# Three reordered steps and a new placement of TensorE's operands in a two-layer graph network kernel

## What is computed

```python
h = relu(layernorm(x))
# layer 0: attention over the graph, then K = 3 hops
Xw = h @ Wv + bv
e  = leaky_relu((Xw @ aw[:d])[:, None, :] + (Xw @ aw[d:])[:, :, None] + ab, 0.2)
A  = adj * exp(e);  T = A / (A.sum(-1, keepdims=True) + 1e-12)
H  = h @ Wk[0] + (T h) @ Wk[1] + (T T h) @ Wk[2] + bk.sum(0)
x  = x + relu(H)
# layer 1: three graph convolutions
h = relu(layernorm(x))
y = relu(adj @ (h @ W1) + b1)
y = relu(adj @ (y @ W2) + b2)
x = x + adj @ (y @ W3) + b3
```

## The kernel before

| product | what moves | starts at | stationary | starts at |
|---|---|---|---|---|
| z1 | m | 0 | w_gcn0 | 64 |
| p2 | w_p2, 258 columns wide | 0, 32 (second half 8, 40) | h0T | 64 |
| z3 | s3 | 0 | adjT | 64 |
| ay | y1 | 0 | aT | 0 |
| s2, s3 | w_gcn1, w_gcn2 | 64 | y | 0 |
| p01 | w_p01 | 64 | h0T | 64 |
| z2 | adjT_full | 64 | s2 | 0 |
| ap | p2, 258 columns wide | 0, 32, 64, 96 | aT | 0 |
| m | adjT_full | 64 | h1 | 64 |

## Time and profile before

### The profile page before, as it was taken

The page is one execution under the profiler, slowest core; times in us unless marked ns, Lnnn a source line. Parts: engine busy times, 40 slices in busy tenths (PEclk is TensorE's granted clock), DMA queues, the critical chain, the costliest instruction groups (busy, mean ns, idle before and its releaser), DMA issues.

```text
span 865.4 us, 21032 instructions
## 1 busy us (share of the span) xinstructions
PE 846.4 (98%) x6236; PEld 794.7 (92%) x6236; DVE 728.3 (84%) x2001; ACT 683.7 (79%) x1671; POOL 509.3 (59%) x593
## 2 busy tenths in 40 slices
PE   6899999999999999999999999999999999999996
PEld 5799999999999999999999999999999999999995
DVE  4788888888888888888888888888888888888872
ACT  4688888888888888888888887887888888888773
POOL 3555655655655655665665665665665665665652
PEclk9999999999999999999999999999999999999999
DMA  8153343343343443443343344334334334334101
GB/s 201 35 119 80 98 99 84 97 97 82 99 97 81 101 95 82 100 96 87 96 95 91 93 94 94 89 94 93 91 94 98 87 92 100 84 94 99 45 25 37
DMA packets 245488, 78.19 MB, mean 90 GB/s; under 512 B 202368, under 2 KB 237312, under 8 KB 245376
## 3 DMA queue, kind: packets, MB, share of 16 engines
q1 hardware_dynamic: 244288, 75.81, 37.2%
q10 hardware_dynamic: 1088, 1.05, 0.4%
HBM read 44.04 MB, written 32.77 MB: 89 GB/s over the span
## 4 chain that ended last, share of the span: by engine, by line
PE 94%; DMA 1%; POOL 1%; issue 1%; DVE 1%; ACT 1%; SPq 0%; ACTq 0%; DVEq 0%; POOLq 0%
PE bank L950 45%; PE bank_p L950 35%; PE bank_turned L950 7%; PE bank_T L950 5%; PE bank_T L971 2%; DMA w_raw<-in_L_gnn_Wk 1%; POOL w_gcn_lo L420 0%; DMA h_blocks<-h_rows 0%; PE bank_p L1127 0%; POOL w_p_lo L415 0%; POOL rstd L376 0%; SPq L307 0%; SPq L286 0%; DVE y_full L767 0%; ACT y_full L604 0%
## 5 line engine op out<-in xcount | busy, mean ns | idle before, releaser
L385 POOL TENSOR_TENSOR y__lo<-y_full,y__hi 128x256 fp32r<-128x256 f32 x256 | 183.3, 736 | 159.6 <-ACT y_full L604 159.6
L376 POOL TENSOR_TENSOR rstd<-veps,minus_half 128x2 f32<-128x2 f32 x128 | 111.5, 871 | 180.2 <-DVE veps L682 174.0
L950 PE MATMUL bank_p<-w_p_hi,h0T_hi 128*128 128x258 f32 (+1 forms) x512 | 175.7, 359 | 1.0 <-ACT h0T_hi L502 0.7
L950 PE MATMUL bank_p<-w_p_lo,h0T_hi 128*128 128x258 f32 (+1 forms) x512 | 165.0, 338 | 0.0
L950 PE MATMUL bank_p<-w_p_hi,h0T_lo 128*128 128x258 f32 (+1 forms) x512 | 141.8, 338 | 0.0
L950 PE MATMUL bank<-w_gcn_hi,y__hi 128*128 128x256 f32 x512 | 130.9, 291 | 1.6 <-ACT y__hi L604 1.3
L950 PE MATMUL bank<-w_gcn_lo,y__hi 128*128 128x256 f32 x512 | 124.7, 279 | 0.0
L604 ACT ACTIVATE y__hi<-bank,bias_col 128x256 fp32r<-128x256 f32 x256 | 119.6, 467 | 3.0 <-PE bank L950 3.0
L604 ACT ACTIVATE y_full<-bank,bias_col 128x256 f32<-128x256 f32 x256 | 120.4, 470 | 0.0
L950 PEld LDWEIGHTS bank_p<-w_p_hi,h0T_hi 128*128 128x128 f32 x512 | 96.6, 189 | 7.1 <-ACT h0T_hi L502 0.9
L950 PEld LDWEIGHTS bank_p<-w_p_lo,h0T_hi 128*128 128x128 f32 x512 | 96.8, 189 | 5.8
(11 more groups left out here) (95 smaller groups left out, 2300.2 us busy)
## 6 DMA issues: line engine op xcount, KB each, us to landing
x_in<-in_x SPq DMA_DIRECT2D x64, 256.0 KB, 3.1
x_new<-x_out SPq DMA_DIRECT2D x64, 256.0 KB, 2.2
h_rows<-h SPq DMA_DIRECT2D x61, 256.0 KB, 2.0
h_blocks<-h_rows SPq DMA_DIRECT2D x244, 64.0 KB, 2.5
adj_blocks<-in_adj SPq DMA_DIRECT2D x256, 32.0 KB, 2.0
w_raw<-in_L_gnn_Wk ACTq DMA_DIRECT2D x3, 256.0 KB, 7.1
w_raw<-in_L_gnn_W SPq DMA_DIRECT2D x3, 256.0 KB, 6.2
bk_bc<-in_L_gnn_bk SPq DMA_DIRECT2D x1, 384.0 KB, 5.9
```

The lines of the kernel that those rows point to most:

```text
L376: pool.tensor_tensor(rstd[n][k % 2][:], veps[n][k % 2][:], minus_half[:], ALU.pow)\
L385: pool.tensor_tensor(y[n][1][:, c], y_full[n][:, c], plain(y[n][0][:, c]), ALU.subtract)\
L950: return pe.matmul(dst, stationary, moving, start=start, stop=stop, skip_group_check=True)
```

## The change

It moves steps in three engines' `one`, and it allocates SBUF in another order. Semaphores and their waits, the instructions and their sizes stay the same.

- GpSimd: `adjT_low` goes from the end of the iteration (for pair i) to behind `power(1, b)`, one iteration later for the same pair.
- ScalarE: `norm(b)` goes ahead of `aT_high(a)`.
- VectorE: `p2_low(a)`, which stood between the wait and the work of `moments(1, b)`, goes behind `guard_variance(1, b)`; `shift(1, b)` goes ahead of `attention(a)`; `turn_adj` is done one pair ahead, behind `finish(d)`, just before `guard_sum(a)`.
- SBUF: every tensor that moves through TensorE in a product starts at 0 modulo 128 bytes, every stationary one at 64. w_p2 and p2 are padded from 258 to 288 columns (`WIDE`), so that their halves start there too; the products still read 258. Two unused tensors fill up to the boundaries, and `scratch`, an output nobody reads, gives its room away (the dot products write into `x_out`'s buffers, early on).

```diff
+WIDE = D + P // 4
...
         ident = sb("ident", [P, P])
+        sb("up_to_a_kilobyte", [P, 3 * P // 4])
...
+        w_gcn = [None] + [hilo(f"w_gcn{n}", [P, C, D]) for n in range(1, K)]
+        w_p01 = hilo("w_p01", [P, C, 2 * D])
+        y1 = slots_hilo(2, "y1_", [P, G, D])
+        m = hilo("m", [P, C, G, P])
+        s3 = hilo("s3", [P, G, D])
+        adjT_full = [sb(f"adjT_full{n}", [P, G, P]) for n in range(4)]
+        w_p2 = hilo("w_p2", [P, C, WIDE])
+        p2 = slots_hilo(2, "p2_", [P, G, WIDE])
+
+        sb("half_a_block", [P, P // 8])
+        w_gcn[0] = hilo("w_gcn0", [P, C, D])
+        h0T = slots_hilo(2, "h0T", [P, G, C, P])
+        s2 = sb("s2", [P, G, D])
+        y = [hilo(f"y{n}_", [P, C, G, P]) for n in range(2)]
+        h1 = [sb(f"h1_{n}", [P, G, D]) for n in range(2)]
+        aT = slots_hilo(2, "aT", [P, G, P])
+        adjT = slots_hilo(4, "adjT", [P, G, P])
...
                 if b is not None:
                     power(1, b, k - LAG_B)
+                    adjT_low(b, (k - LAG_B) % ROUND)
...
-                if (n := here(i, 0)) is not None:
-                    adjT_low(n, k)
...
-                if a is not None:
-                    aT_high(a, k)
                 if b is not None:
                     norm(b, kb)
+                if a is not None:
+                    aT_high(a, k)
...
-                    moments(1, b, kb, lambda: p2_low(a, k) if a is not None else None)
+                    moments(1, b, kb, lambda: None)
                     guard_variance(1, b, kb)
-                elif a is not None:
+                if a is not None:
                     p2_low(a, k)
-                if a is not None:
+                if second(i):
                     turn_adj(a, k)
-                if a is not None:
-                    attention(a, k)
                 if b is not None:
                     shift(1, b, kb)
+                if a is not None:
+                    attention(a, k)
...
                     finish(d, kd)
+                if nxt is not None:
+                    turn_adj(nxt, kn)
```

More of the change, by code:

```diff
@@ L68, in gnn_kernel, with slots_hilo @@
         ident = sb("ident", [P, P])
+        sb("up_to_a_kilobyte", [P, 3 * P // 4])
+        def slots_hilo(n, name, shape):
+            return [hilo(f"{name}{s}", shape) for s in range(n)]
+        w_gcn = [None] + [hilo(f"w_gcn{n}", [P, C, D]) for n in range(1, K)]
[14 more added lines that the diff above has]
+        adjT = slots_hilo(4, "adjT", [P, G, P])
         w_raw = sb("w_raw", [P, 2 * K, C, D])
         wv_raw = sb("wv_raw", [P, C, D])
-        w_p2 = hilo("w_p2", [P, C, D + 2])
-        w_p01 = hilo("w_p01", [P, C, 2 * D])
-        w_gcn = [hilo(f"w_gcn{n}", [P, C, D]) for n in range(K)]
         wva = sb("wva", [P, C, 2])
@@ L129, in gnn_kernel @@
         x1 = slots(2, "x1_", [P, G, D])
-        m = hilo("m", [P, C, G, P])
-        s2 = sb("s2", [P, G, D])
-        s3 = hilo("s3", [P, G, D])
         y_full = [sb(f"y_full{n}", [P, C, G, P]) for n in range(2)]
-        y = [hilo(f"y{n}_", [P, C, G, P]) for n in range(2)]
         def bank(name):
@@ L630, in one @@
                     p1_copy(a, k, 0)
+                if b is not None:
+                    norm(b, kb)
                 if a is not None:
                     aT_high(a, k)
-                if b is not None:
-                    norm(b, kb)
                 if c is not None:
@@ L832, in dot @@
             def dot(dst, a, b, junk, signal):
[L834 removed]
+                dve.tensor_tensor_reduce(x_out[junk // G][:, junk % G, :], a, b, 1.0, 0.0, ALU.mult, ALU.add, dst)\
                    .then_inc(signal, 1)
@@ L899, in one @@
                     x1_statistics(b, kb)
-                    moments(1, b, kb, lambda: p2_low(a, k) if a is not None else None)
+                    moments(1, b, kb, lambda: None)
                     guard_variance(1, b, kb)
-                elif a is not None:
+                if a is not None:
                     p2_low(a, k)
-                if a is not None:
+                if second(i):
                     turn_adj(a, k)
+                if b is not None:
+                    shift(1, b, kb)
                 if a is not None:
                     attention(a, k)
-                if b is not None:
-                    shift(1, b, kb)
                 if i == 1:
@@ L988, in h_low_ready, with times_weights @@
                     pe.wait_ge(hT_lo, i - ON_TENSOR + 1)
-            def times_weights(hT, rows, w, dst, starts, passes=(False, True)):
+            def times_weights(hT, rows, w, cols, dst, starts, passes=(False, True)):
                 steps = [(g, c, a, b) for low in passes for g in range(G) for c in range(C)
@@ L995, in times_weights @@
                     start = c == 0 and a == HI and b == HI and g in starts
-                    last = matmul(dst[g], rows(hT[a], g, c), w[b][:, c, :], start, a == LO and c == C - 1)
+                    last = matmul(dst[g], rows(hT[a], g, c), w[b][:, c, 0:cols], start, a == LO and c == C - 1)
                 return last
@@ L1003, in p2_product @@
                     h_low_ready(i)
-                    times_weights(h0T[k % 2], graph_first, w_p2, dst, range(G), (True,)).then_inc(p2_done, 1)
+                    times_weights(h0T[k % 2], graph_first, w_p2, D + 2, dst, range(G), (True,)).then_inc(p2_done, 1)
                     return
@@ L1010, in p2_product @@
                     pe.wait_ge(y1_made, i)
-                times_weights(h0T[k % 2], graph_first, w_p2, dst, range(G), (False,))
+                times_weights(h0T[k % 2], graph_first, w_p2, D + 2, dst, range(G), (False,))
             def p01_product(i, k, g, chunks=range(C)):
@@ L1036, in ap_product @@
                     for g in range(G):
-                        last = matmul(bank_p2[:, g, 0:D + 2], aT[k % 2][a][:, g, :], p2[k % 2][b][:, g, :],
+                        last = matmul(bank_p2[:, g, 0:D + 2], aT[k % 2][a][:, g, :], p2[k % 2][b][:, g, 0:D + 2],
                                       (a, b) == (HI, HI), a == LO)
```

18 lines of the change are left out of this document (4 added, 14 removed).

## The result

The changed kernel takes **843.65 us** (median of 4 runs, 841.58 to 845.46). The kernel before, run beside it, takes 866.88 (4 runs, 865.77 to 868.97). The ratio is 0.973, with a 95% interval of 0.970 to 0.976. The forecast was 845.

A forecast was written before the change was run, and what follows sets the result against it. TensorE, busy all 12.92 us of an iteration, was the bound, then a ring through aT_hi and ap. Saving 0.17 (s3's wait) and 0.19 (placement) gave 12.56 us; 22.0 us over 61 iterations gave 845 us, range 820 to 861.

The forecast's parts named there:

- the ring: Chain hb, variance, norm, aT_hi, ap, m, s3, z1, p2, z3, ay, hb, forecast to bound the iteration at 12.56 us.
- The cost of nothing: GpSimd: moved `adjT_low` (0.73) falls into 2.44 us of idle time, so it costs nothing.
- `stats` at 1.88: VectorE: `stats` starts 1.88 us after `hb`, starting the times that put `nshift` at 3.96 and ap at 5.82.
- s2's wait: TensorE in s2 waits 0.24 us for y's low part; it goes, but merely becomes a wait for `aT_hi`.
- s3's wait: TensorE in s3 waits 0.17 us for y's low part; it goes, since that part comes 0.30 sooner.
- The term of 0.39: TensorE: opposite 64-byte halves for operands speed up fp32r matmuls by 0.39 us an iteration, 0.19 of it in the ring.
- no ring: Rival: the ring does not close, so TensorE's full 0.80 us an iteration counts; 818 us, chance 0.12.
- no placement: Rival: the new SBUF starts do nothing, so only 0.17 us an iteration is saved; 856 us, chance 0.18.
- a slack of about 0.6 against 0.7: Attention branch: `aT_hi` comes 0.7 us later where slack was about 0.6; the argument against "no ring".
- everything: Rival: placement gives its full gain, the ring saves 0.67 and the second ring, saving 0.63, binds; 829 us, chance 0.14.
- the second ring: Ring through y's low part and s3's low pass, saving 0.30 + 0.15 + 0.18 (28 matmuls), 0.63 us.
- Slower: Rival: GpSimd's `rstd` stretches by 0.38 us beside `p_lo`; 867 us (0.06), or 879 us without placement gain (0.05).

The follow-up runs named there:

- `adjT_low` beside `x`: Kernel before with `adjT_low` moved only to directly behind y's first two low parts, ahead of `power`, so still running beside `x`: 866.68 us, ratio 1.000.
- the moves alone: Kernel before with the step moves on GpSimd, ScalarE and VectorE, but the old SBUF allocation: 845.04 us, ratio 0.973.

## Why the prediction was right, and where it was not

The number was right, 845 against 843.65, and so was the period, 12.56 against 12.54. That is in part luck: two of its steps were wrong by about as much, in opposite directions (0.24 and 0.19 an iteration, some 15 and 12 us), and the ring that it made the bound isn't the bound.

- *GpSimd.* The cost of nothing held; `adjT_lo` lies in idle time. What failed is the step that left `x`'s duration as it was: "`stats` at 1.88". It stands at 405.34 - 403.70 = 1.64, because y's low part is no longer beside `x`. This was in the rows read: the prediction reckoned with just that contention for `rstd`, 1.07 beside VectorE's low part of y1 and 0.69 alone, but not for VectorE's own step. `aT_hi` came at 5.05 instead of 5.35, 0.24 of it from `x` and 0.06 from hand-overs a little shorter than worked out, and ap at 5.58 instead of 5.82 (its own hand-over of 0.47 was 0.53).
- *s2's wait.* It was to become a wait of about 0.4 for `aT_hi`. With `x` at 0.69 it did not: ap stands 0.24 earlier, just the wait removed, and what remains ahead of ap is 0.044, measured by taking it away. Here TensorE does gain s2's wait. The idea behind the step, that a wait ahead of the ring's end is worth nothing, is right where `x` keeps its length: `adjT_low` beside `x` shows that, only at s3 and not at ap.
- *s3's wait.* 0.17 gone, as forecast, but with more room: `y__hi` at 5.36, not 5.67.
- *VectorE.* The aggregate, the guarded variance and `rstd` at 0.69 came as forecast. `nshift` at 3.68 instead of 3.96, 0.24 of that `x`'s. Idle 0.20 for `rstd` (0.3 forecast) and 0.24 for `aT_hi` (0.6 forecast). `alpha` stretches to 0.69 beside `adjT_lo`, which costs nothing as long as `aT_hi` stands behind `norm`. With `aT_hi` first, `norm` waits for it too, up to 0.26 an iteration by these rows.
- *Placement.* The term of 0.39 (0.19 of it in the ring) was mis-sized. It read ay's 0.120 against z1's 0.113 as the halves, and s2's 0.118 as an exception; s2 was the case that should have decided. Between the moves alone and the changed kernel the products other than ap shrink by 0.037 together (s2 0.032, p2 0.008 and ay 0.007 less, z3 0.006 more), and ap gives 0.027 of it back to its wait: 0.010 net.
- *The sum.* The ring forecast at 12.56, corrected by 0.24 for `x` and by 0.19 for the placement, is 12.51. TensorE's work before without its two waits is 12.93 - 0.41 = 12.52. Measured: 12.54. So two rivals came true together, no ring (0.12) and no placement (0.18). Each alone stood at 818 or 856; together they give 866.6 - 61 x 0.41 = 842. The prediction kept them apart and had no price for both at once. Against "no ring" it held a slack of about 0.6 against 0.7; its own rows give 5.82 - 0.47 - 4.66 = 0.69, so that argument carried little. In "everything" the second ring has 36 matmuls of this kind, not 28 (s3's last 4, z1 12, p2 8, z3 6, ay 6), and saves 0.68; the first ring's 0.67 would bind, at 826 instead of 829.
- *Slower.* `rstd` did not stretch beside `p_lo`. The Trainium skill (SBUF — State Buffer, "Who interferes with whom") has a VectorE step outside its 2-port modes contend with GpSimd only where it reads two inputs from SBUF, and then with a GpSimd step that reads SBUF. Most rows agree: `p_lo` (one input in PSUM) leaves `rstd` at 0.69, while `x` and `alpha` (two in SBUF) take 0.94 and 0.69 beside GpSimd's subtractions and 0.69 and 0.43 alone. But `alpha` keeps its 0.43 beside `rstd` in the kernel before, and `veps`, with one input, takes 0.28 beside `x1b` and 0.17 alone; the prediction's "only" left out the 2-port modes, and whether `veps` runs in one no row shows. The same section has TensorE's two read ports independent and TensorE waiting on no other engine, and nothing on where the two operands start. By a shift of 64 bytes between them the runs differ, 853.1 against 843.65 us.

An order slower than the kernel before does exist: GpSimd's and ScalarE's moves without VectorE's, 883.5 us.

## What to carry to other kernels

A wait that shows on the bounding engine is worth what the whole ring allows, not its length: s2's was worth nothing in the kernel before and about 0.15 an iteration in the changed one. Compute the ring through every engine, and test a removal by looking for the wait's reappearance further on. When a step moves on one engine, go through the other engine's steps that ran beside it, before and after, and re-price those too; here 13 of the 23 us hung on one step's duration. Test reordered steps together and with one left out at a time, since in part they may gain nothing or lose.

## What the runs showed of the hardware

- A step that has to share with the other engine waits for that engine's step to end; the two don't merely slow each other. In the kernel before `x` (two inputs in SBUF, 128x512 float32) ends 0.55 behind y's second low part in each of 46 steady iterations, whether 0.31 or 0.40 of that was left when `x` began, so it takes 0.86 to 0.95 instead of 0.69. Beside `adjT_lo` it ends 0.55 behind that. `alpha` (128x256) ends 0.28 behind `adjT_lo`, alone it takes 0.43; GpSimd's `rstd` ends 0.56 behind VectorE's y1 low part, alone 0.69. In all three an overlap costs its length less 0.13 to 0.15.
- Streams of fp32r matmuls with 256 columns and a weight load each hold 0.113 or 0.118 with the same operands in the same places (0/64 or 64/0 modulo 128 bytes); at equal starts (0 or 64) they go at 0.118 to 0.120, unevenly. 512 columns: 0.229 at 0/64, 0.232 to 0.233 at equal starts and at 64/0. What sets the pace is open.
- A matmul whose low operand comes late costs more than the wait: where s2 waits, the three steps after the first take 0.46 instead of 0.34.
